# Experts' outputs scattered tile by tile to token order, and loaded plainly at the end

## The reference, cut to what matters

```
x = x + L0_xattn(layernorm(x), ctx);  x = x + L0_ffn(layernorm(x))
x = x + L1_xattn(layernorm(x), ctx);  x = x + L1_ffn(layernorm(x))

def L1_ffn(x_, up, gate, down, router, w_up_s, w_gate_s, w_down_s):
    idx = argmax(x_ @ router.T)                       # one expert of 8 for each token
    h = silu(einsum('bc,ehc->ebh', x_, gate)) * einsum('bc,ehc->ebh', x_, up)
    y = sum over e of (h @ down[e].T) * onehot(idx)   # 512 hidden, 256 out
    ys = silu(x_ @ w_gate_s.T) * (x_ @ w_up_s.T) @ w_down_s.T
    return y + ys
```

## Time and profile before

| what | value |
|---|---|
| median of three runs | 2613.51 us |
| the profiled execution, its own time | 2618.82 us |
| its span, first to last instruction | 2616.9 us |
| TensorE busy | 2520.7 us, 96% |
| VectorE, ScalarE, GpSimd busy | 80%, 48%, 57% |
| last stage: issue of its first tile load | 2460.1 us |
| last copy of `y` begins | 2588.1 us |
| first gather begins | 2590.5 us |

### The profile page before, as it was taken

How to read it: one execution, slowest core, us unless ns; L and a number is a source line. 1 busy time by engine, 2 the same in 40 slices (tenths; PEclk the granted TensorE clock), 3 DMA queues, 4 the chain that set the end, 5 groups by cost and what they waited for, 6 DMA issues and landing times. The chain is left out here.

```text
span 2616.9 us, 37958 instructions
## 1 busy us (share of the span) xinstructions
PE 2520.7 (96%) x13304; PEld 1776.5 (68%) x13304; DVE 2091.2 (80%) x2602; ACT 1246.1 (48%) x1774; POOL 1482.1 (57%) x1124
## 2 busy tenths in 40 slices
PE   8999999999999889999999899999999999998795
PEld 6666565656665678888888766666666665656684
DVE  7888888888888487777777788888888888866695
ACT  5555555555554323333333355455555454533393
POOL 5878777877777311111111187687878777760345
PEclk9999999999999999999999999999999999999897
DMA  4122212222221200000000121222131222115112
GB/s 147 45 59 53 63 45 58 63 49 50 63 51 41 72 19 24 24 24 24 24 24 18 47 75 45 55 61 59 45 79 45 59 53 55 45 29 235 47 54 88
DMA packets 118648, 145.09 MB, mean 55 GB/s; under 512 B 63856, under 2 KB 80112, under 8 KB 117488
## 3 DMA queue, kind: packets, MB, share of 16 engines
q1 hardware_dynamic: 113664, 136.10, 19.3%
q0 software_dynamic: 1536, 4.20, 0.5%
q10 hardware_dynamic: 3312, 3.02, 0.3%
HBM read 80.93 MB, written 11.80 MB: 35 GB/s over the span
## 5 line engine op out<-in xcount | busy, mean ns | idle before, releaser
L326 POOL TENSOR_TENSOR L1a_psums<-L1a_psums,L1a_probs 128x512 f32<-128x512 f32 x384 | 479.1, 1293 | 0.0
L326 POOL TENSOR_TENSOR L0a_psums<-L0a_psums,L0a_probs 128x512 f32<-128x512 f32 x384 | 478.8, 1289 | 0.0
L530 DVE TENSOR_REDUCE L1a_row_max<-psum 128x2 f32<-128x2048 f32 x128 | 293.6, 2293 | 59.2 <-PE psum L796 58.9
L530 DVE TENSOR_REDUCE L0a_row_max<-psum 128x2 f32<-128x2048 f32 x128 | 293.5, 2293 | 57.7 <-PE psum L796 57.2
L400 ACT ACTIVATE L0a_probs<-psum 128x1024 f32<-128x1024 f32 x256 | 251.6, 1027 | 105.9 <-PE psum L819 105.7
L400 ACT ACTIVATE L1a_probs<-psum 128x1024 f32<-128x1024 f32 x256 | 251.6, 1027 | 105.1 <-PE psum L819 104.9
L1168 DVE SCALAR_TENSOR_TENSOR xres<-psum,L0e_weights_of,xres 128x256 f32<-128x256 f32 x544 | 225.6, 478 | 22.6 <-PE psum L1379 21.7
L833 PE MATMUL psum<-L1a_probs,L1a_v 128*64 128x512 f32 x1024 | 240.5, 601 | 0.0
L833 PE MATMUL psum<-L0a_probs,L0a_v 128*64 128x512 f32 x1024 | 240.4, 601 | 0.0
L1365 PE MATMUL psum<-xnT_hi,L0e_w_hi 128*128 128x512 f32 x544 | 215.0, 395 | 9.4 <-DVE L0e_hid L1176 9.4
L1365 PE MATMUL psum<-xnT_lo,L0e_w_hi 128*128 128x512 f32 x544 | 214.6, 394 | 0.0
(11 more groups left out here) (384 smaller groups left out, 6148.6 us busy)
## 6 DMA issues: line engine op xcount, KB each, us to landing
L0a_k_hs<-L0a_k_st SPq DMA_DIRECT2D x64, 256.0 KB, 3.6
L1a_k_hs<-L1a_k_st SPq DMA_DIRECT2D x64, 256.0 KB, 3.7
L0a_raw<-in_attention SPq DMA_DIRECT2D x33, 384.0 KB, 3.4
L1a_raw<-in_attention SPq DMA_DIRECT2D x33, 384.0 KB, 3.4
L1weights<-in_sorted SPq DMA_DIRECT2D x2, 6144.0 KB, 20.6
L0a_q_hh<-L0a_q_hh SPq DMA_DIRECT2D x64, 128.0 KB, 2.3
L1a_q_hh<-L1a_q_hh SPq DMA_DIRECT2D x64, 128.0 KB, 2.3
ctx_stage<-in_experts SPq DMA_DIRECT2D x19, 384.0 KB, 3.0
```

Source lines behind the costliest of these rows:

```text
L326: nc.gpsimd.tensor_tensor(psums[:, h, :], a, probs[:, h, kv, :], ALU.add).then_inc(sem["acc"], 1)
L530: nc.vector.reduce_max(row_max[:, qt, 0:33:32], psum[:, 0:4 * BANK].rearrange("p (h k) -> p h k", h=2), axis=AX.X).then_inc(sem["max"], 1)
```

## The change

- The rows of `sorted_x` get one more column (257 numbers, `WIDE`). It holds the number of the token; in the slots that no token has, 2,048 plus the partition. GpSimd writes these numbers with two iotas, in `rows` and in `zeros`, and they travel with the wipe and with the 16 scatters.
- In `sorted_phase` GpSimd copies the last column of each loaded tile to integers (`token`), and when `y` of that tile is ready, scatters it by these numbers to `expert_out` in DRAM, which is in token order (with 128 rows more for the slots without a token). ScalarE's store to `sorted_y` is gone.
- SP's load of tile u waits for this copy of tile u-2 too, since it overwrites the buffer. VectorE's copy to `y` waits until GpSimd has passed on that the scatter two tiles before has landed (`yfree`).
- After the last tile SP waits for all scatters, and loads `expert_out` back in four plain DMAs of 512 KB. The additions wait for these four, and the four stores of the output no longer wait for each other.

GpSimd's and SP's functions are written out for all 23 tiles instead of looping. Per step GpSimd now holds: `tokens(u)`, `low_down(u-1)`, `free(u-3)`, `store_rows(u-2)`.

```diff
-        sorted_x = nc.dram_tensor("sorted_x", (TILES * P, DIM), F32, kind="Internal").ap()
-        sorted_y = nc.dram_tensor("sorted_y", (TILES * P, DIM), F32, kind="Internal").ap()
+        sorted_x = nc.dram_tensor("sorted_x", (TILES * P, WIDE), F32, kind="Internal").ap()
+        expert_out = nc.dram_tensor("expert_out", (TOK + P, DIM), F32, kind="Internal").ap()
...
+                            nc.gpsimd.iota(rows[:, :, DIM], pattern=[[P, NT]], base=0, channel_multiplier=1,
+                                           allow_small_or_imprecise_dtypes=True).then_inc(sem["token"], 1)
...
-                            nc.gpsimd.memset(zeros[:, :], 0.0).then_inc(sem["zero"], 1)
+                            nc.gpsimd.memset(zeros[:, 0:DIM], 0.0).then_inc(sem["zero"], 1)
+                            nc.gpsimd.iota(zeros[:, DIM:WIDE], pattern=[[0, 1]], base=TOK, channel_multiplier=1,
+                                           allow_small_or_imprecise_dtypes=True).then_inc(sem["zero"], 1)
...
                     @block.sync
                     def _(sp):
-                        def load(r, u):
-                            sp.wait_ge(sem["xt"], r * 2 + (u + 1))
-                            sp.dma_start(xs[:, u % 2, :], tile(x_slots, r, u)).then_inc(sem[f"xs{u % 2}"], 16)
...
+                        def load(u):
+                            sp.wait_ge(sem["xt"], u + 1)
+                            sp.wait_ge(sem["token"], u + 1)
+                            sp.dma_start(xs[:, u % 2, :], x_slots[u, :, :]).then_inc(sem[f"xs{u % 2}"], 16)
...
+                        for par in range(2):
+                            sp.wait_ge(sem[f"y{par}"], 16 * ((TILES + 1 - par) // 2))
+                        for part in range(OUTS):
+                            sp.dma_start(rows[:, part * n:(part + 1) * n, 0:DIM], expert_tiles[:, part * n:(part + 1) * n, :])\
+                                .then_inc(back[part], 16)
                         for part in range(OUTS):
                             sp.wait_ge(sem["sum"], n * (part + 1))
                             sp.dma_start(store[:, part * n:(part + 1) * n, :], xres[:, part * n:(part + 1) * n, :])\
                                 .then_inc(sem["out"], 16)
-                            sp.wait_ge(sem["out"], 16 * (part + 1))
+                        sp.wait_ge(sem["out"], 16 * OUTS)
...
                     @block.gpsimd
                     def _(pool):
-                        def step(r, u):
-                            if there(r, u - 1):
-                                w = expert(nc.gpsimd, r, u - 1)
-                                pool.wait_ge(sem["dhi"], r * 2 + u)
-                                nc.gpsimd.tensor_tensor(down_lo[:, (u - 1) % 2, :], w(DOWN_COLS), down_hi[:, (u - 1) % 2, :],
-                                                        ALU.subtract).then_inc(sem["dlo"], 1)
-
-                        run(pool, step)
-                        for par in range(2):
-                            pool.wait_ge(sem[f"y{par}"], 16 * ((TILES + 1 - par) // 2 + 1))
-                        for t in range(NT):
-                            nc.gpsimd.indirect_dma_start(rows[:, t, :], None, sorted_y,
-                                                         bass.IndirectOffsetOnAxis(ap=slot_of[:, t:t + 1], axis=0))\
-                                .then_inc(back[t], 16)
+                        def tokens(u):
+
+                            pool.wait_ge(sem[f"xs{u % 2}"], 16 * (u // 2 + 1))
+                            nc.gpsimd.tensor_copy(token[:, u:u + 1], xs[:, u % 2, DIM:WIDE]).then_inc(sem["token"], 1)
+
+                        def low_down(u):
+                            w = expert(nc.gpsimd, 0, u)
+                            pool.wait_ge(sem["dhi"], u + 1)
+                            nc.gpsimd.tensor_tensor(down_lo[:, u % 2, :], w(DOWN_COLS), down_hi[:, u % 2, :], ALU.subtract)\
+                                .then_inc(sem["dlo"], 1)
+
+                        def store_rows(u):
+                            pool.wait_ge(sem["token"], 2 + u + 1)
+                            pool.wait_ge(sem["ycopy"], 2 + u + 1)
+                            nc.gpsimd.indirect_dma_start(expert_out, bass.IndirectOffsetOnAxis(ap=token[:, u:u + 1], axis=0),
+                                                         y[:, u % 2, :], None).then_inc(sem[f"y{u % 2}"], 16)
+
+                        def free(u):
+
+                            pool.wait_ge(sem[f"y{u % 2}"], 16 * (u // 2 + 1))
+                            pool.sem_inc(sem["yfree"], 1)
+
+                        pool.sem_inc(sem["token"], 2)
+                        pool.sem_inc(sem["yfree"], 2)
+                        tokens(0)
+                        for u in range(1, TILES + 2):
+                            if u < TILES:
+                                tokens(u)
+                            if u - 1 < TILES:
+                                low_down(u - 1)
+                            if u >= 3:
+                                free(u - 3)
+                            if u >= 2:
+                                store_rows(u - 2)
...
-                            if there(r, u - 3):
-                                act.wait_ge(sem["ycopy"], k + u)
-                                act.dma_start(tile(y_slots, r, u - 3), y[:, (u - 3) % 2, :]).then_inc(sem[f"y{(u - 3) % 2}"], 16)
...
-                                dve.wait_ge(sem[f"y{u % 2}"], r * 16 + 16 * (u // 2))
+                                dve.wait_ge(sem["yfree"], k + (u - 1))
...
-                            dve.wait_ge(back[t], 16)
-                            nc.vector.tensor_tensor(xres[:, t, :], xres[:, t, :], rows[:, t, :], ALU.add).then_inc(sem["sum"], 1)
+                            dve.wait_ge(back[t // (NT // OUTS)], 16)
+                            nc.vector.tensor_tensor(xres[:, t, :], xres[:, t, :], rows[:, t, 0:DIM], ALU.add).then_inc(sem["sum"], 1)
```

More of the change, by code:

```diff
@@ L994, in expert_phase @@
                                         for a in (eq, scores, start))
-                    tiles, end = (sb(s, tag + n, [P, E]) for n in ("tiles", "end"))
+                    tiles, end = (spare[:, n:n + E] for n in (P, P + E))
                     past = late[:, :].rearrange("p (t e) -> p t e", e=E)
@@ L1451, in _, with sorted_phase @@
                         down(ROUNDS - 1, ROUND - 1)
-        def sorted_phase(tag, weights, loaded, place, rows, xres, store):
-            slot_of, expert_of = place
+        def sorted_phase(tag, weights, loaded, expert_of, rows, xres, store):
             per = HID // P
             assert 2 * KD * HID == TOK and KD == 2
+            expert_tiles = expert_out[0:TOK, :].rearrange("(t p) d -> p t d", p=P)
             x_slots = sorted_x.rearrange("(t p) d -> t p d", p=P)
-            y_slots = sorted_y.rearrange("(t p) d -> t p d", p=P)
             with scope() as s:
-                xs = sb(s, tag + "xs", [P, 2, DIM])
+                xs = sb(s, tag + "xs", [P, 2, WIDE])
+                token = sb(s, tag + "token", [P, TILES], I32)
                 xsT_hi = sb(s, tag + "xsT_hi", [P, 2, KD * P], F32R)
@@ L1477, in sorted_phase @@
                 y = sb(s, tag + "y", [P, 2, DIM])
-                sem = sems(s, tag, "xs0 xs1 xt xhi xlo ghi glo dhi dlo gu silu mul ht hhi hlo down ycopy y0 y1 sum out")
-                back = [s.enter_context(nc.semaphore(f"{tag}back{n}")) for n in range(NT)]
+                sem = sems(s, tag, "xs0 xs1 xt xhi xlo ghi glo dhi dlo gu silu mul ht hhi hlo down ycopy y0 y1 yfree token sum out")
                 OUTS = 4
+                back = [s.enter_context(nc.semaphore(f"{tag}back{n}")) for n in range(OUTS)]
                 LOOP = (TILES - 4) // 2
@@ L1543, in _ @@
                     @block.scalar
                     def _(act):
-                        for par in range(2):
-                            act.sem_inc(sem[f"y{par}"], 16)
                         for part in loaded:
@@ L1691, in build @@
             expert_phase("L1e_", cfg, None, w["experts"], xres, (rows, *place), (load(0), load(1)))
-            sorted_phase("L1s_", weights, loaded, place, rows, xres, out_tiles)
+            sorted_phase("L1s_", weights, loaded, place[1], rows, xres, out_tiles)
 def kernel(**inputs):
```

27 lines of the change are left out of this document (13 added, 14 removed).

## The result

| | before | changed | 
|---|---|---|
| median, four runs each on one chip | 2613.31 us (2611.55 to 2613.93) | 2639.23 us (2638.29 to 2641.66) |
| ratio, with its 95% interval | | 1.0102 [1.0084, 1.0119] |
| the profiled execution, and its span | 2618.82 us, 2616.9 us | 2638.29 us, 2636.6 us |
| forecast | | 2622 us, range 2608 to 2634 us |

The change costs 25.9 us. The forecast had the sign, and 8.7 us; the time lies outside its range.

A forecast was written before the change was run, and what follows sets the result against it. TensorE, busy 96% of the span, was taken as the bound. Late tile loads and the loop's end, 18.7 us together, less 10.0 us at the end gave +8.7 us on the 2613.51 us median: 2622 us, range 2608 to 2634 us.

The forecast's parts named there:

- the chain named, station by station: Last stage: transposes of tile n-2 through GpSimd's split, scatter and CAST to tile n's load, 11.66 us; 17.3 us over 19 turns.
- The load in time: Rival, last stage: tile loads still come in time, turns stay 4.92 us, only the end moves; 2605 us, 12%.
- the new gap in a turn is 0.9 us: Last stage: TensorE stands 0.9 us in each turn, stretching it from 4.92 to 5.83 us.
- The clock was a rival: Last stage: TensorE's clock falls to 1.2 GHz after each gap, products take about twice 4.9 us; past 2690 us, 2%.
- the prediction's signs of being right: Last stage: tile waits in nearly every turn, turns of 5.6 to 6.0 us, TensorE about 85% busy, end 18 to 21 us.
- VectorE beside the scatter, 0.4 us: Last stage: VectorE's weight splits, both operands in SBUF, delay GpSimd's scatter, adding 0.4 us to the two-turn chain.
- the rival in which both halves come first: Last stage: GpSimd waits behind both VectorE splits, giving turns of 6.43 us; 2634 us, 14%.
- The end of the loop, +1.4 us: Last two tiles: a scatter between GpSimd's two weight splits delays the last down product by 1.4 us.
- The end, -10.0 us: After the last copy of y: one scatter and four plain loads replace 16 gathers, saving 10.0 us.
- The wait for yfree, at nothing: Last stage: VectorE's copy of y waits for the scatter two tiles back; 2.5 us of cover, so no cost.
- The CAST at 0.15 us: Last stage: GpSimd's one-column copy of token numbers takes 0.15 us, a value near a one-column MEMSET's 0.10 us.
- The wider rows: Rows of 1,028 bytes: no cost, tile loads landing in 2.0 us; estimated six transactions instead of four per row.

The follow-up runs named there:

- e1: The changed kernel with three buffers instead of two for the tiles' rows, TensorE's function written out: 2609.83 us, ratio 0.9968 to the kernel before.
- e2: The changed kernel with GpSimd's copy of a tile's token numbers one step earlier, two buffers kept: 2607.58 us, ratio 0.9962 to the kernel before.
- e8: The changed kernel with eight identity transposes before TensorE's tile wait, for the first nine tiles only, loop written out: 2622.28 us, ratio 1.0042 to before.
- e4: The changed kernel with the number copy directly behind GpSimd's split and ahead of the scatter: 2623.27 us, ratio 1.0017 to the kernel before.
- e5: The changed kernel with VectorE's gate and up weight splits cut to 128 columns, part of the products not correct: 2619.43 us, ratio 1.0010 to before.
- e3: The changed kernel with eight identity transposes on TensorE ahead of each wait for a tile: 2628.85 us, ratio 1.0037 to the kernel before.
- e7: The changed kernel run once more, unaltered: 2640.28 us, ratio 1.0081 to the kernel before; one of six executions took 2624.1 us.

## Why the prediction was wrong

**The direction, and the place.** The loads of tiles come late by the chain named, station by station, and that decides: e1 cuts it by a third buffer, e2 by an earlier number, and each gives back all of the loss. The load in time was a rival there, priced at 2605 us, that is 8.5 us below before; e1 and e2 came out 8.8 and 11.0 us below theirs. The condition was judged rightly, and so was its price.

**The step that failed: the wait of two turns was shared evenly between them, "the new gap in a turn is 0.9 us".** From this came turns of 5.83 us at full clock and 2% for the clock. The runs showed one wait of 2.2 us in every second turn, mostly with a fall of the clock behind it, and 13.60 us for a pair instead of 11.66 us. The sum by stations:

| station | forecast | measured | 
|---|---|---|
| transposes, gate and up | 3.03 | 4.64 |
| SiLU to GpSimd's start | 2.02 | 2.07 |
| split on GpSimd | 2.41 | 2.41 |
| 0.17 and scatter, with 0.4 for VectorE | 1.53 | 1.97 |
| gap and CAST | 0.45 | 0.30 |
| SP, landing, TensorE's start | 2.22 | 2.21 |
| sum | 11.66 | 13.60 |

Of the 1.94 us missing, 1.61 us stand in the station with the lower clock and 0.44 us in the scatter; the rest cancels. In the pair at full clock (12.23 us) the first station is back at 3.03 us, and GpSimd starts 2.32 us behind it instead of 2.07, so the fall costs 1.4 us net.

The missing time of two turns need not be shared between them. Two buffers alternate, and the chain reaches over two turns; one turn can carry the whole wait of the pair, 1.8 us by the forecast's own numbers and 2.2 us as it came. The clock was a rival and got 2%, on a gap of 0.9 us. Its price was wrong as well: not all products of a turn ran at the lower level, but those of some 3.4 us behind a long wait, and the rows of before do not show how long the lower level lasts. With what the traces show the time does come out. From tile 4 to tile 22 the changed kernel takes 15.1 us more than e8: nine pairs of turns at 0.6 us more (12.23 against 11.64 us), and seven falls at 1.4 us. An eighth fall, at the end, cost 1.5 us.

Of the prediction's signs of being right, TensorE's busy share (84% of the pair, about 85% forecast) and the end (19.1 us, 18 to 21) held, but the tiles were waited for in every second turn, not in nearly every one.

**What made it so.** The load of tile n hangs on the transposes of tile n-2. So the even and the odd tiles make two chains, and TensorE's own work sets only the least distance between them. The chain fixes how long two turns take, but not how they share the wait. This is an argument from the waits in the code; the traces agree with it. The pairs were there before the first fall of the clock and behind the last long wait without one, and they were there at full clock in e4 and e5. So the fall does not make the pairs. It comes behind waits that the pairs make long. Two patterns of the changed kernel's loop then differ in cost. Even turns: a wait of 0.7 to 1.0 us in each, the clock 1.00, 5.82 us (e8). Pairs: one wait of 2.2 us, 6.1 us a turn on average at full clock and 6.8 us with the fall. At full clock the pair's extra 0.6 us is the scatter, which now begins within a VectorE split, and GpSimd's later start, less what the CAST saves. With the VectorE splits made short (e5) the pair's wait is 1.3 us and the clock stays. The forecast described the even pattern, and one execution in ten took 2624.1 us, as it would; without a trace that it had this pattern is not shown. What tips an execution into one or the other stays open. In e8 it was work on TensorE around the first nine tiles, or the loop written out with it; e3, where the loop was kept, speaks for the work. Why the clock fell behind seven of these waits and not behind the eighth stays open too.

**The smaller steps.** *VectorE beside the scatter, 0.4 us*: 0.84 us in the pattern that came, since the scatter waited out most of one split; the rival in which both halves come first did not occur. Until e5 this rested on the 1.38 us of one row. The Trainium skill (SBUF — State Buffer, "Who interferes with whom") infers that descriptor writing is not held up by a tensor_tensor; here scatters took 1.80 us beside one and 1.00 us once it was short, so for an indirect scatter the measurement decides. Whether the writing of descriptors waited or the reading of the token numbers from SBUF, no run separates. *The end of the loop, +1.4 us*: measured +2.9 us. The scatter between the last two splits is there (the splits' starts, 3.55 us apart instead of 2.35 us, 1.2 us more), and the gate products of the last tile but one come behind one more long wait, with the clock falling in them (4.36 us instead of 2.81 us), 1.5 us. *The end, -10.0 us*: -9.7 us. SP issued the first load at 2621.5, 4.0 us after the start of the copy of y and not 3.1 us. The forecast had 0.2 us between the copy and the scatter; it was 1.1 us, some 0.8 us of handover and 0.3 us for the scatter before to land. The last of the four, issued at 2623.0, landed 7.8 us later, 9.3 us behind the first issue and not 10.2 us. The two errors cancel. *The wait for yfree, at nothing*: right on VectorE, whose copies of y waited for TensorE alone; but GpSimd's own wait for the landing costs some 0.3 us once, at the last scatter. *The CAST at 0.15 us*: 0.20 us with nothing beside it, up to 1.2 us beside VectorE's splits. *The wider rows*: loads landed in 1.9/2.1/2.3 us against 1.9/2.0/2.5 us; at most 0.1 us. The prediction's estimate of six transactions instead of four was counted wrongly: a row of 1,028 bytes that starts at any multiple of 4 bytes touches five blocks of 256 bytes.

## What to carry to other kernels

Where a wait returns over several turns of a loop with alternating buffers, ask how it spreads over them: all of it may fall on one turn. The gap is then as many times longer as there are turns in the chain, and the question is what the engine did behind gaps of that length. Put a small instruction that frees a buffer ahead of the long ones on its engine, not behind them: here one CAST, one step sooner, is worth 1.2 to 1.4%, 31 to 37 us, and turns a loss of 1.0% into a gain of 0.4%. And two steady patterns of one loop can lie some 15 us apart; a few executions, or a single trace, need not show both.

## What the runs showed of the hardware

- The granted clock of TensorE fell behind waits of 2.2 to 2.6 us that came once in 13.6 us (0.53 to 0.59 over the next 3.4 us, seven times in the changed kernel), and again behind seven such waits in e7 (0.50 to 0.59). It stayed at 1.00 behind one wait of 2.29 us in the changed kernel and one of 2.13 us in e7, and behind the waits of e5 (1.3 us once in 11.3 us, 1.9 us at most), of e4 (1.1 us once in 11.1 us, 1.4 us at most) and of e8 (0.7 to 1.0 us in every turn of 5.8 us). So a wait of over 2 us brought the fall in most cases, and its length alone does not decide.
- An indirect scatter of 128 rows of 1 KB takes 0.96 to 1.01 us of GpSimd, and about 1.80 us when it starts within a VectorE split with two inputs in SBUF (2.04 us at most, in e4); the pair of VectorE's splits takes 2.68 us instead of 2.36 us then. A CAST of one column takes 0.20 us, and up to 1.2 us in such a place.
- A scatter landed 2.4 to 2.5 us after its issue in e3, where each took GpSimd 1.0 us. In e1 and e2, where most took 1.80 us, the median was 3.2 us. The last but one of the changed kernel took 3.56 us to land, though GpSimd had it for 0.99 us only.
- In GpSimd's function `free` stands ahead of `store_rows`, so each scatter waits for the landing of the one before it. A version without this wait was not tried.
